# Two up banks, normalisation on ScalarE and a shorter ranking in the first stage of a two-layer transformer kernel

## The reference, cut to what matters

```python
x = x + cos_sim(_layernorm(x) @ Wv.T + bv, ctx @ Wt.T + bt)   # 32 x 128 tokens, C = 128
h = _layernorm(x)                                             # first stage: these lines
s = sigmoid(h @ gate_w) + gate_bias                           # 8 experts in 4 pairs
keep the 2 best pairs (by the sum of s in a pair), then the 2 best experts; w = 2.5 * s / sum
x = x + sum_e w_e * ((silu(h @ w_gate[e]) * (h @ w_up[e])) @ w_down[e]) + shared expert
x = x + cross_attention(_layernorm(x), ctx)                   # later stages, not touched
x = self_attention_and_experts(x)
```

## Time and profile before

| | us |
|---|---|
| Median of 3 runs (lowest, highest) | 955.29 (953.72, 956.67) |
| The profiled execution, its own time | 956.91 |
| Its span in the profile | 954.9 |
| First stage (to the last L506) | 256.4 |
| Busy in the span: PE, DVE, ACT, POOL | 751.5, 661.3, 395.2, 227.0 |

### The profile page before, as it was taken

The page is one execution under the profiler, slowest core; times in us unless marked ns, Lnnn a source line. Parts: engine busy times, 40 slices in busy tenths (PEclk is TensorE's granted clock), DMA queues, the critical chain, the costliest instruction groups (busy, mean ns, idle before and its releaser), DMA issues. The chain is left out here.

```text
span 954.9 us, 26276 instructions
## 1 busy us (share of the span) xinstructions
PE 751.5 (79%) x10100; PEld 556.5 (58%) x10100; DVE 661.3 (69%) x1809; ACT 395.2 (41%) x746; POOL 227.0 (24%) x366
## 2 busy tenths in 40 slices
PE   3579889887637887888888428778764999999998
PEld 2345555554415665666676305556554788888886
DVE  4478888986446887888888347888644656666653
ACT  2122122222113554555555325566532554555553
POOL 4333333320083022201000475335001111111100
PEclk9958898978956999999999658999995999999999
DMA  3000000520112211221110000000000000000000
GB/s 93 20 20 21 18 4 17 129 40 11 23 46 77 70 42 41 69 71 52 50 53 13 9 0 4 3 5 4 3 4 2 1 13 11 11 11 11 11 11 12
DMA packets 33081, 26.41 MB, mean 28 GB/s; under 512 B 9740, under 2 KB 29912, under 8 KB 32984
## 3 DMA queue, kind: packets, MB, share of 16 engines
q1 hardware_dynamic: 29944, 24.07, 9.5%
q10 hardware_dynamic: 3040, 0.98, 0.4%
HBM read 13.51 MB, written 7.34 MB: 22 GB/s over the span
## 5 line engine op out<-in xcount | busy, mean ns | idle before, releaser
L1777 PEld LDWEIGHTS bank<-w2r,hme 128*128 128x128 f32 x1024 | 132.1, 191 | 16.3 <-ACT hme L1618 2.1
L1777 PE MATMUL bank<-w2r,hme 128*128 128x128 f32 x1024 | 135.6, 276 | 0.5 <-DVE Xq L1720 0.5
L1618 ACT ACTIVATE hme<-bank,b 128x512 f32<-128x512 f32 x128 | 86.6, 688 | 95.8 <-PE bank L97 95.7
L785 ACT ACTIVATE P<-bank 128x512 f32<-128x512 f32 x128 | 76.8, 600 | 95.9 <-PE bank L956 95.8
L1720 DVE SCALAR_TENSOR_TENSOR Xq<-bank,wgte,Xq 128x128 f32 (+1 forms) x256 | 72.0, 344 | 51.9 <-PE bank L1777 38.4
L886 DVE TENSOR_SCALAR bank<-bank 128x512 f32<-128x512 f32 x128 | 89.0, 696 | 27.0 <-PE bank L947 26.9
L894 DVE TENSOR_REDUCE mx<-bank 128x4 f32<-128x512 f32 x128 | 87.1, 681 | 1.4 <-PE bank L939 1.2
L956 PE MATMUL bank<-mT,negsel 128*128 128x128 f16 x512 | 51.0, 223 | 44.5 <-DVE bank L886 41.9
L350 ACT ACTIVATE sg<-bank 128x512 f32<-128x512 f32 x40 | 23.9, 598 | 128.2 <-PE bank L581 99.0
L956 PEld LDWEIGHTS bank<-mT,negsel 128*128 128x128 f16 x512 | 32.1, 99 | 55.5 <-issue 40.9
L767 POOL TENSOR_TENSOR inv_sum<-inv_sum,dn 128x16 f32<-128x16 f32 x32 | 7.1, 221 | 203.2 <-DVE dn L915 203.2
(11 more groups left out here) (376 smaller groups left out, 1787.6 us busy)
## 6 DMA issues: line engine op xcount, KB each, us to landing
cross_q<-qh SPq DMA_DIRECT2D x24, 128.0 KB
K<-cross_k SPq DMA_DIRECT2D x96, 32.0 KB
Q<-cross_q SPq DMA_DIRECT2D x8, 384.0 KB, 3.6
X<-in_x SPq DMA_DIRECT2D x8, 256.0 KB, 2.8
Xq<-X SPq DMA_DIRECT2D x32, 64.0 KB
cross_k<-kh SPq DMA_DIRECT2D x16, 128.0 KB
Yq<-Y SPq DMA_DIRECT2D x32, 64.0 KB
out_x<-Xq SPq DMA_DIRECT2D x32, 64.0 KB, 1.7
```

Of the source, the lines that this page charges most:

```text
L785: act.activation(P[j][:], TB[j % 2][:], ACT.Exp, scale=SCALE).then_inc(s["p_ready"], 1)
L1618: act.activation(hm[:, p % HR], UP[p % RING][:], ACT.Gelu_apprx_tanh, bias=b1[:, p:p + 1]).then_inc(s["gelu"], 1)
L1777: last = pe.matmul(Y[e % 2][:, cols], hm[:, p % HR, cols], w2r[:, p], start=(p % 2 == 0 and i == 0), stop=(p % 2 == 1), skip_group_check=True)
```

## The change

The banks are P0, P1, PB, one gate bank GP and two up banks. PE computes gate, signals `g_psum`, computes up into bank k % 2, signals `u_psum`, and does not wait for eT there. The pick has its own signal `w_psum` and its place behind `prep` and `route`. The normalisations go to ACT as scale times x plus bias, for which POOL adds a negated mean and a product; they stand in place p = 0 of the next step, behind the SiLU. Ranking subtracts and compares the difference with a mask of 0 or -2e-38 (with it, an equal value of lower index counts); the last reduce stays. All loops over groups in this stage are written out.

```diff
-GATE_STEPS = 20
+GATE_STEPS = 18
...
-        P0, P1, PB, G0, G1, UP, WB, DN = bank
-        GP = [G0, G1]
+        P0, P1, PB, GP, U0, U1, WB, DN = bank
+        UP = [U0, U1]
...
         def sweep(eng, step):
-            for g in range(-3, 1):
-                step(g)
-            with eng.Fori(1, G - 3) as g:
-                step(g)
-            for g in range(G - 3, G):
+            for g in range(-3, G):
                 step(g)
...
-            over_groups(sp, load, 0, G - 1)
+            for g in range(G):
+                load(g)
...
-            pool.memset(before4[:], 1.0)
-            pool.memset(before8[:], 1.0).then_inc(s["consts"], 1)
+            pool.memset(before4[:], -2e-38)
+            pool.memset(before8[:], -2e-38).then_inc(s["consts"], 1)
...
-                pool.wait_ge(s["eps" + k], g + 1)
-                pool.tensor_tensor(rs[k][:, 1, :], rs[k][:, 0, :], half[:, 0:GB], ALU.pow).then_inc(s["rs" + k], 1)
+                pool.tensor_scalar(rs[k][:, 2, :], mv[k][:, :, 0], -1.0, None, ALU.mult).then_inc(s["eps" + k], 1)
+                pool.wait_ge(s["eps" + k], 3 * g + 2)
+                pool.tensor_tensor(rs[k][:, 1, :], rs[k][:, 0, :], half[:, 0:GB], ALU.pow).then_inc(s["eps" + k], 1)
+                pool.wait_ge(s["eps" + k], 3 * g + 3)
+                pool.tensor_tensor(rs[k][:, 3, :], rs[k][:, 2, :], rs[k][:, 1, :], ALU.mult).then_inc(s["rs" + k], 1)
...
+            def normalise(k, g):
+                act.wait_ge(s["rs" + k], g + 1)
+                for i in range(GB):
+                    last = act.activation(xn[k][:, i, :], xg(g)[:, i, :], ACT.Identity, bias=rs[k][:, 3, i:i + 1],
+                                          scale=rs[k][:, 1, i:i + 1])
+                last.then_inc(s["xn" + k], 1)
...
-                        act.wait_ge(s["gu_psum"], k + 1)
-                        after(act, s["hm_ready"], before(k, p) + 1)
-                        act.activation(sg[:, p % 2, :], GP[p % 2][:], ACT.Silu).then_inc(s["sg_ready"], 1)
+                        act.wait_ge(s["g_psum"], k + 1)
+                        after(act, s["hm_ready"], k - 1)
+                        act.activation(sg[:, k % 2, :], GP[:], ACT.Silu).then_inc(s["sg_ready"], 1)
+                    if p == 0 and has(g + 2):
+                        normalise("A", g + 2)
+                    if p == 0 and has(g + 1):
+                        normalise("B", g + 1)
...
-                    tie = mask.unsqueeze(1).broadcast_to(shape)
-                    dve.tensor_tensor(room[:, 0], other, own, ALU.is_gt)
-                    link(dve.tensor_tensor(room[:, 1], other, own, ALU.is_equal))
-                    link(dve.tensor_tensor(room[:, 2], room[:, 1], tie, ALU.mult))
-                    link(dve.tensor_tensor(room[:, 1], room[:, 0], room[:, 2], ALU.add))
+                    least = mask.unsqueeze(1).broadcast_to(shape)
+                    link(dve.tensor_tensor(room[:, 0], other, own, ALU.subtract))
+                    link(dve.tensor_tensor(room[:, 1], room[:, 0], least, ALU.is_gt))
...
                         dve.wait_ge(s["sg_ready"], k + 1)
-                        after(dve, s["down_psum"], k - NBLK + 1)
+                        dve.wait_ge(s["u_psum"], k + 1)
...
+                            dve.wait_ge(s["w_psum"], (NBLK - 1) * g + p + 1)
+                            after(dve, s["down_psum"], k - NBLK + 1)
                             dve.tensor_tensor(hm[:, p, :], su[:, i, :], WB[:], ALU.mult).then_inc(s["hm_ready"], 1)
...
-                        if has(g + 3):
-                            normalise("A", g + 3)
-                        if has(g + 2):
-                            normalise("B", g + 2)
...
             def up(g, p):
                 k = NBLK * g + p
+                x = [tok(t, g) for t in xT]
+                after(pe, s["sg_ready"], k)
+                split_product(pe, GP[:], [w[:, 0, p, :] for w in w0], x).then_inc(s["g_psum"], 1)
+                after(pe, s["hm_ready"], k - 1)
+                split_product(pe, UP[k % 2][:], [w[:, 1, p, :] for w in w0], x).then_inc(s["u_psum"], 1)
+
+            def weight(g, p):
                 if p == 0:
                     pe.wait_ge(s["eT_ready"], g + 1)
...
                 if p < NBLK - 1:
-                    last = pe.matmul(WB[:], pick[:, p, :], tok(eT, g), start=True, stop=True)
-                last.then_inc(s["gu_psum"], 1)
+                    after(pe, s["hm_ready"], NBLK * g + p)
+                    pe.matmul(WB[:], pick[:, p, :], tok(eT, g), start=True, stop=True).then_inc(s["w_psum"], 1)
...
                     if has(g):
+                        weight(g, p)
                         down(g if p >= 2 else g - 1, (p - 2) % NBLK)
```

More of the change, by code:

```diff
@@ L155, in layer0 @@
         mv = {k: sb("mv" + k, [128, GB, 2]) for k in "AB"}
-        rs = {k: sb("rs" + k, [128, 2, GB]) for k in "AB"}
+        rs = {k: sb("rs" + k, [128, 4, GB]) for k in "AB"}
         half = sb("half", [128, 8])
@@ L186, in layer0 @@
             stB mvB epsB rsB xnB xBT_psum xB_hi xB_lo logit_psum th_ready gate_step carrier wst_ready eT_psum eT_ready
-            gu_psum sg_ready su_ready hm_ready down_psum x2_ready layer1_loaded"""
+            g_psum u_psum w_psum sg_ready su_ready hm_ready down_psum x2_ready layer1_loaded"""
         s = room.sems(names)
@@ L379, in stats @@
                 last.then_inc(s["mv" + k], 1)
[L381 to L387, removed]
             steps = 0
@@ L475, in step @@
                     if has(g):
-                        i = p % 2
+                        i = k % 2
                         dve.wait_ge(s["sg_ready"], k + 1)
-                        after(dve, s["down_psum"], k - NBLK + 1)
+                        dve.wait_ge(s["u_psum"], k + 1)
                         if p < NBLK - 1:
-                            dve.tensor_tensor(su[:, i, :], sg[:, i, :], UP[:], ALU.mult).then_inc(s["su_ready"], 1)
+                            dve.tensor_tensor(su[:, i, :], sg[:, i, :], UP[i][:], ALU.mult).then_inc(s["su_ready"], 1)
                             dve.wait_ge(s["su_ready"], (NBLK - 1) * g + p + 1)
+                            dve.wait_ge(s["w_psum"], (NBLK - 1) * g + p + 1)
+                            after(dve, s["down_psum"], k - NBLK + 1)
                             dve.tensor_tensor(hm[:, p, :], su[:, i, :], WB[:], ALU.mult).then_inc(s["hm_ready"], 1)
                         else:
-                            dve.tensor_tensor(hm[:, p, :], sg[:, i, :], UP[:], ALU.mult).then_inc(s["hm_ready"], 1)
+                            after(dve, s["down_psum"], k - NBLK + 1)
+                            dve.tensor_tensor(hm[:, p, :], sg[:, i, :], UP[i][:], ALU.mult).then_inc(s["hm_ready"], 1)
                     if has(g + 2):
```

## The result

The changed kernel takes 960.56 us in the median (957.81 to 964.44, 10 runs), the kernel before 954.16 us beside it (950.39 to 958.83, 10 runs): a ratio of 1.0068, 95% interval 1.0041 to 1.0095. The forecast was 953.5 us, a slightly faster kernel, with a range of its own from 949.5 to 958. The profiled execution took 961.94 us, its span is 959.9.

What follows compares the result with a forecast made beforehand. No engine is full; one chain through the engines bounds each period. Run-in +2.6, five periods -0.5, run-out -4.4, lower clock +0.5 make -1.8 against the 955.3 us median: 953.5 us, own range 949.5 to 958, 8 in 10 947 to 962.

Steps and rivals of the forecast that it cites:

- The circle: One chain through all engines per period, from block 2's `hm` to the next, 26.15 us; only work on it counts.
- Segments 1, 3 and 7: Block 2's `hm` to L548, 3.61 to 3.5; `wm` to statistics B, 5.65 to 4.83; gate to `hm`, 6.04 to 5.50.
- segment 2: L548 to `wm`: 2.00 to 3.04 us at half clock or 1.9 at full, through waiting for the late pick.
- The last two Ds: Ends of block 2's `hm` in the last two groups: 13.0 us apart against 17.45, with two up banks.
- the run-out: Stage part after the five periods, 49.52 us: 4.4 less with two up banks, 0.5 back for a lower clock.
- segments 5 and 6: Normalisation to block 0's `hm`, 2.44 to 3.27 us (ScalarE normalises, pick); then to the gate, 4.62 to 4.28.
- lets the clock fall there more often: TensorE's idle time ahead of the transposes grows from some 1.3 to 2.1 us; 0.1 us a period added.
- The slower rival: Picks wait behind half-clock work in every period: periods of 28.2 us, kernel 963.5 us; chance 0.17.
- segment 4: Statistics to normalisation: 1.79 to 2.10 us, GpSimd's longer root less 0.17 for constant waits.
- keeps inside B's wait: Root A, ahead of root B in GpSimd's queue, grows too but was to just fit within B's wait.
- The run-in: Stage part before the five periods, 75.79 us: three passes pay 0.9 each, +2.6 with ranking's gain (bounds +1 and +5).
- the first D: End of the first block 2 `hm` at the run-in's close, forecast at 78.4 us.

Runs made afterwards that it cites:

- e3: Changed kernel with normalisations back on VectorE, the short root, and the pick right behind the up product: 931.7 us, 0.978 of the kernel before.
- e4: Kernel before with only the stage's loops written out and the short ranking: 938.4 us, 0.986 of the kernel before.
- e6: Kernel before with only the ranking in three operations: 949.0 us, 0.997 of the kernel before.
- e1: Changed kernel with normalisations back on VectorE and the short root on GpSimd, late pick kept: 939.3 us, 0.986 of the kernel before.
- e7: Changed kernel with eight more products, results unused, on TensorE ahead of the transposes of A: 949.5 us, 0.996 of the kernel before.
- e9: Kernel of e1 with GpSimd's two extra root operations kept, their results unused: 950.9 us, 1.000 of the kernel before.
- e5: Kernel before with only the stage's loops written out: 942.7 us, 0.989 of the kernel before.
- e2: Changed kernel with the pick sent right behind the up product again: 952.1 us, 0.998 of the kernel before.
- e10: Kernel of e3 with six more products, results unused, on TensorE ahead of L548: 933.3 us, 0.981 of the kernel before.

## Why the prediction was wrong

**What was right.** The circle is what binds, VectorE's load is not: 15.6 us left it and the periods grew. Segments 1, 3 and 7 came within 0.03 us, segment 2 within 0.1. Four normalisations took 1.65 us (forecast 1.6). The last two Ds are 12.7 us apart (forecast 13.0), the run-out gained 5.4 (forecast 3.9), and e3 against e4 shows the banks' share of the run-out, 40.6 against 46.8 (with the pick's own signal). The ranking's 2.7 to 3 us in it (e4, e6) were not foreseen, and the late pick takes 2.2 back (e1 against e3).

**The step that failed** is the sum of the period, in its segments 5 and 6. I priced TensorE's work from the transposes on at full clock and added 0.1 us for "lets the clock fall there more often". At the transposes of B it fell in every period: L556 0.91 to the next start in place of 0.49, the pick 0.43 in place of 0.22, the down product 1.7 in place of 0.9, and the up product behind it partly slow. That is 0.66 us in segment 5 (4.02 against e7's 3.36) and 1.4 in segment 6 (5.59 against 4.22), 2.0 a period and 10 of the stage. e7 shows it: the products that it adds change only what TensorE did before the transposes, and the other segments stay within 0.1 us. The gap that I foresaw was 2.1 us; it was 1.6 to 2.75. The slower rival named this mechanism, its period of 28.2 (measured 28.3) and its gain in the run-out; it had a chance of 0.17. That it comes so close is in part luck. It had L548 slow each time, and L548 was at full rate in three of five periods, so segment 2 was 2.43 and not its 3.04; the longer root, which it did not have, gave 0.3 of that back, and segments 5 and 6 came 2.06 over their sums, where it had 1.7.

**A term that was mis-sized** is the root in segment 4: 0.4 foreseen per root, 0.61 measured (1.91 against 1.30, with constant waits), since the negated mean runs behind the first operation with a distance of 0.28 and not beside it. And "keeps inside B's wait" was wrong: with B's statistics 1.51 us behind the start of root A, root B waits for root A. So segment 4 is 2.40 in place of 2.10: 1.42 with the short root (e1), 0.61 for the longer one and 0.37 for this wait. The run-in grew by 3.9 in place of 2.6, and it was split wrongly: 1.2 was for GpSimd and 1.5 for ScalarE, but e9, with the long root and the normalisation on VectorE, has the first D at 79.6, 4.3 later than e1, and ScalarE adds 0.1. Why the roots of three passes cost 4.3 there was not traced.

Two small sums of the working don't come out. The terms given for segment 4 make 2.00, not 2.10 (1.79 + 0.1 + 0.28 - 0.17), and four ACTIVATEs of 0.29 with overlap make 0.83, not 1.0. Neither changes the outcome.

**The rule of the Trainium skill** (TensorE: Matmul & The Clock Gate, Part 4: PE-mode transpose) was that transposes don't keep the clock up. The runs do not settle it: in e7 the transposes are at full speed behind dense products, and in e1 and e4 they are at full speed behind gaps of 1.2 to 1.7 us. In the changed kernel L556 is slow each time, which agrees with it, but no run here changes the transposes and leaves the gaps.

**A second size was wrong,** though the forecast does not rest on it. Loops and ranking were to give 0.9 us a period in segments 1, 3 and 7 of e4, some 4 in all, and gave 11.5. Of the 2.3 us a period, segments 1, 3, 4 and 7 have 1.3, segment 2 has 0.4 and segment 6 has 0.6. The last is the clock: L556 was slow in two of five periods before and in none of e4. The forecast of the changed kernel took segments 1, 3 and 7 at 3.5, 4.83 and 5.50, which both e4 and the changed kernel measure within 0.03, and segment 6 at full clock. So it had this gain in it, and erred in taking the clock as it was.

**The balance of the stage.** Before to e4, -14.4 (loops and ranking); e4 to e3, -4.8 (two up banks, early pick); e3 to e1, +4.3 (late pick); e1 to e9, +14.5 (long root); e9 to the changed kernel, +9.3 (ScalarE normalises, 0.5 us longer, with the late place): +8.9. The order of the steps matters, as the late pick costs 7.5 in the last place. By the medians the same steps are -1.4%, -0.8, +0.8, +1.4 and +0.7, so direction and order of size hold; the steps under 5 us are near what one profile can tell. How the 9.3 divide between ScalarE's time and a firmer fall of the clock was not tried.

## What to carry to other kernels

When no engine is full, an operation that moves off the busiest engine is worth what it takes off the chain, and a small operation added to that chain costs its own time and the idle time that it makes for TensorE. Price the clock with it: read how long TensorE stands idle ahead of the chain's matmuls and at which speed they ran after such gaps, and take the half-clock price into the range wherever the change lengthens a gap past those. A gap's length alone does not settle it, as the next section shows. Test a bundle part by part: here loops, ranking and banks were worth 19 us of the stage together (e3), and the move of the normalisation cost 21 to 24.

## What the runs showed that I had not expected

Writing a loop out gave 1.1% by itself (e5, interval 0.6 to 1.6). The profile has 7.5 of the 10.5 us in the stage; of the 1.5 us a period, 0.6 are L556 at full speed each time, and 0.9 lie in the other segments, where the waits are shorter. The other 3 us are not explained.

At the transposes longer idle time goes with a slow L556, but the two gaps ahead of L523 and L556 do not decide alone. With 1.16 and 0.44 us it is at full speed in all periods of e4, with 2.2 us and more ahead of L523 it is slow in all seven periods of the changed kernel and of e9 that have such a gap. In between the runs disagree. With 1.67 and 0.44 us it is at full speed (e1), with 1.35 and 0.45 slow (e2), and in the kernel before 1.3 and 0.7 us gave 0.89 and 1.11 in two periods and 0.66 in this one:

```profile
166.45 0.65 PE L523 MATMUL bank<-ident,xnA 128*128 128x128 f32 x4 [1.30 <-DVE xnA L385]
...
168.26 0.66 PE L556 MATMUL bank<-ident,xnB 128*128 128x128 f32 x4 [0.72 <-DVE xnB L385]
```

What else decides was not tried.

Filler products can pay: 1.7 us of useless work in a gap of up to 2.75 us gave back 2.2 us a period (e7), while the same ahead of L548 cost more than it gave (e10).
